# Attention and FP4 feed-forward on one core: who adds the partial denominators, and where the maximum enters the scores

## The chip, the cores and the metric

The kernel runs on one core of one Trainium2 chip. The metric is the device time of one execution in microseconds (us); lower is better. An execution has four engines that compute side by side, each with its own instruction stream: TensorE (PE in the profile, PEld for its weight loads), VectorE (DVE), ScalarE (ACT) and GpSimd (POOL). SyncE (SP) starts transfers. The streams meet only at semaphores: a wait such as `pe.wait_ge(p_ready, n)` holds back its own engine and everything queued behind it there.

## The reference, cut to what matters

```python
x = x + attention(layernorm(x))      # x is 1 x 2048 x 128, 16 heads of 64
x = x + ffn(layernorm(x))            # FP4 fake quantisation in blocks of 16, inner width 352
# attention:
sim  = einsum('bhid,bhjd->bhij', q, k) / 8
attn = softmax(sim, axis=-1)
out  = einsum('bhij,bhjd->bhid', attn, v)
```

All of it is float32. The change touches the softmax alone: its row maximum, which is subtracted before the exponential, and its denominator.

## The kernel before, in words

**Units.** The attention is cut into 32 units: 8 pairs of heads by 4 chunks of 512 queries. A unit has 16 steps j, one for each tile of 128 keys. The program text has 8 units (`BODY`), numbered w; they are run 4 times (`ITERS`), the last time with `last` set, and then without the projections for a next pair of heads and with parts of the feed-forward's quantisation in their place.

**A step.** PE makes the scores of 128 keys by 512 queries for two heads in one of the two buffers of `s_ps` (`scores`, L982 to L997), ACT takes the exponential of them into one of four buffers `probs` (L590), and PE multiplies these by V into `o_ps` (`weighted`, L1136). The scores come from split operands, three products for each of the two heads, and each product of a head uses 64 rows of the array; the two heads use different halves of it. The keys are held as differences to the tile two before, so a score buffer is not cleared within a unit: step j adds the difference to what step j-2 left. Only steps 0 and 1 (j < `BACK`) start a buffer, and there two products of a matrix of ones with `spread` add minus the row maximum, over all 128 rows of the array (L995). `spread` is a diagonal form of `neg_max`, written by DVE at L775 in step 13 for the unit after.

**Maxima.** Beside this, PE makes scores for the maxima of the unit ahead (`row_maxima`, L1002 and L1009, 64 rows for each of the two heads), ACT takes their positive part (`rise`, L510) and DVE folds both into `part_max` (`max_slot`, L766). Each of these has one buffer, so that PE's next `row_maxima` waits for DVE's last `max_slot` (`mx_free`) and ACT's last `rise` (`mx_rise`).

**Denominator.** POOL adds the probabilities of tiles 0 to 12 in 12 additions (L476) into `acc_pool`, DVE those of tiles 13 to 15 in two (L901, L906) into `acc_dve`. In step 1 of the next unit (`K_AT`) DVE adds the two into `acc_dve` (`sum_tiles`, L807), and in step 5 PE sums them over the partitions with a matrix of ones (`den`, L1118). The reciprocal (L784), the normalisation (L792), the output projection (L1126) and its addition to `y` (L799) follow.

**Order.** Every engine's order is written by hand. PE's is the loop at L1161 to L1177: in even steps `row_maxima` and then the scores of step j+1; in odd steps these scores and then `row_maxima`, then the projection due in this step (`misc`), then `weighted` for steps j-1 and j. In step 15 the scores are those of step 0 of the next unit. DVE's is the loop at L857 to L906, POOL's at L466 to L481. In the last four units POOL also scales inputs of the quantisation (`over_scale`, L452, after its additions; `times_scale`, L462), for which ACT waits in step 2 of the following unit (`sizes`, L570) and DVE supplies the factors (`block_scales`, L741, in step 15). ACT waits in each step for a free buffer of `probs`, that is for POOL's addition of four tiles before (`pool_free`).

Of the kernel before, what the change touches and what calls it, by code (L numbers as in the profile page):

```python
# [31 lines left out]
DH = 64  # L32
# [22 lines left out]
Q_BUFS = 4  # L55
# [84 lines left out]
def block_kernel(nc, x_in, w_qkv, w_out, b_out, w_gate, w_up, w_down, out):  # L140
    ctx = ExitStack()
    with ctx:
# [162 lines left out]
        def par(w):  # L305

            return (w // CHUNKS) % 2
# [94 lines left out]
        def _(pool):  # L402
# [36 lines left out]
                               ALU.add).then_inc(biased, 1)  # L439

            pool.wait_ge(dt_ready, CHUNKS)
            pool.memset(acc_dve[:, 1, :, :], 1.0).then_inc(dve_adds, DVE_ADDS - 1)
            pool.memset(acc_pool[:, 1, :, :], 0.0).then_inc(dve_adds, 1)
            pool.sem_inc(pool_adds, START)

            def over_scale(n):
                src, _dst, width = quantised(n)
# [17 lines left out]
            def body(it, last):  # L465
                for w in range(BODY):  # L466
                    acc = acc_pool[:, w % 2, :, :]
                    for j in range(1, POOL_TILES):
                        if j == 1:

                            pool.wait_ge(den_acc, after(it, 1, w))
                        else:
                            pool.wait_ge(pool_adds, after(it, POOL_ADDS, w, j - 1))
                        pool.wait_ge(p_ready, after(it, STEPS, w, j + 1))
                        first = probs[:, 0, :, :] if j == 1 else acc
                        pool.tensor_tensor(acc, first, probs[:, j % P_BUFS, :, :], ALU.add) \  # L476
                            .then_inc(pool_adds, 1)
                        if last and w > CHUNKS and j == 9:
                            times_scale(w - CHUNKS - 1)
                    if last and w >= CHUNKS:  # L480
                        over_scale(w - CHUNKS)  # L481

# [171 lines left out]
        def _(dve):  # L654
# [144 lines left out]
                dve.tensor_tensor(yc, yc, misc_ps[:, :].rearrange("p (t d) -> p t d", t=TQ), ALU.add) \  # L799
                    .then_inc(misc_free, 1)  # L800

            def sum_tiles(it, w):

                sums = acc_dve[:, (w - 1) % 2, :, :]
                dve.wait_ge(pool_adds, after(it, POOL_ADDS, w))
                dve.wait_ge(dve_adds, at(it, DVE_ADDS, w, DVE_ADDS))
                dve.tensor_tensor(sums, sums, acc_pool[:, (w - 1) % 2, :, :], ALU.add).then_inc(den_acc, 1)  # L807

            def split_weights(i, count):

                dve.wait_ge(wqkv_high, count)
# [42 lines left out]
            def body(it, last):  # L854
                for w in range(BODY):
                    sums = acc_dve[:, w % 2, :, :]
                    for j in range(STEPS):  # L857
# [3 lines left out]
                        if j == MAX_DONE and runs(last, u, s):  # L861
                            dve.wait_ge(s_ready, at(it, STEPS, w, BACK))
                            neg_maximum(max_no(it, w, j) + 1, at(it, 1, w, 2))
                        if j == K_AT:
                            sum_tiles(it, w)
                        if j == K_AT and not skipped("K", w, last):
                            dve.wait_ge(hi_done, kq_no(it, w, "K", last))
                            k_low(1 - par(w), w % CHUNKS, misc_ps[:, :]).then_inc(misc_free, 1)
# [39 lines left out]
            with dve.Fori(0, ITERS - 1) as it:  # L908
                body(it, False)
            body(ITERS - 1, True)  # L910
            sum_tiles(ITERS - 1, BODY)
            for t in range(TQ):
                invert(ITERS - 1, BODY, True, t)
            normalise(ITERS - 1, BODY, True)
# [41 lines left out]
        def _(pe):  # L956
# [22 lines left out]
                    ins = project_v_tile(ps, i, c, t)  # L979
                return ins  # L980

            def scores(buf, i, q, j, maximum=None):  # L982

                keys = slice(j * P, (j + 1) * P)
                parts = [(k_hi[i][:, keys], q_hi[q]), (k_hi[i][:, keys], q_lo[q]), (k_lo[i][:, keys], q_hi[q])]
                for n, (stationary, moving) in enumerate(parts):
                    for h in range(2):
                        rows = slice(DH * h, DH * (h + 1))
                        ins = pe.matmul(s_ps[:, buf, h, :], stationary[rows, :], moving[rows, :],  # L989
                                        start=(n == 0 and j < BACK), stop=(n == 2 and j >= BACK), skip_group_check=True)  # L990
                if j < BACK:
                    if maximum is not None:
                        pe.wait_ge(spread_ready, maximum)
                    for h in range(2):
                        ins = pe.matmul(s_ps[:, buf, h, :], ones_r[:, :], spread[:, h, :], start=False, stop=True,  # L995
                                        skip_group_check=True)
                return ins  # L997

            def base(h, i, k, q, pair):
# [82 lines left out]
            pe.wait_ge(zeros_ready, ZEROED)  # L1082
            pe.wait_ge(pro_v, CHUNKS)
            pe.wait_ge(pro_lo, len(PRO_LO))
            scores(0, 0, 0, 0, 1).then_inc(s_ready, 1)

            pe.sem_inc(pv_done, P_BUFS)

            def misc(name, it, w, last):
# [5 lines left out]
                if name == "raw":  # L1095
                    ins = project_raw(ps[:, 0:HALF], 1 - par(w), c)
                elif name == "K":
                    if c == 0:
                        pe.wait_ge(wqkv_split, it * 2 + w // CHUNKS + 2)
                    ins = project(ps, 1 - par(w), 1, c, dx_hi, dx_lo)  # L1100
                elif name == "V":
                    ins = project_v(ps, 1 - par(w), c)
                elif name == "Q":
                    ins = project(ps, par(w + 2), 0, (w + 2) % CHUNKS, xhat_hi, xhat_lo)
                elif name == "down":
                    for i, (row, rows) in enumerate(FF_TILES):
                        ins = pe.transpose(ps[0:rows, i * DIM:(i + 1) * DIM], wx[:, 6 * DIM + row:6 * DIM + row + rows],
                                           ident[:, :])
                elif name in ("gate", "up"):
                    pe.wait_ge(f_quant, 1)  # L1110
                    for i, (row, rows) in enumerate(FF_TILES):
                        col = (i if name == "gate" else 3 + i) * DIM
                        ins = pe.transpose(ps[:, row:row + rows], wx[0:rows, col:col + DIM], ident[0:rows, 0:rows])
                elif name == "den":

                    pe.wait_ge(den_acc, after(it, 1, w, 1))
                    for h in range(2):
                        ins = pe.matmul(ps[DH * h:DH * (h + 1), :], ones[:, :], acc_dve[:, (w - 1) % 2, h, :],  # L1118
                                        start=True, stop=True)
                else:  # L1120

                    if c == 1:
                        pe.wait_ge(wo_loaded[par(w)], it * 16 + 16)
                    pe.wait_ge(o_normed, after(it, 1, w, 2))
                    for t in range(TQ):
                        ins = pe.matmul(ps[:, t * P:(t + 1) * P], o_norm[:, t * P:(t + 1) * P], wo[par(w - 1)][:, :],  # L1126
                                        start=True, stop=True)
# [28 lines left out]
            def body(it, last):  # L1156
                for w in range(BODY):
                    ahead = not (last and w == BODY - 1)

                    pe.wait_ge(misc_free, misc_before(it, w, last) + START)  # L1160
                    for j in range(STEPS):  # L1161
                        if j % 2 == 0:
                            row_maxima(it, w, last, j)
                        if j < STEPS - 1:
# [1 line left out]
                            scores((j + 1) % 2, par(w), w % Q_BUFS, j + 1).then_inc(s_ready, 1)  # L1166
                        elif ahead:
                            pe.wait_ge(p_ready, after(it, STEPS, w, j))
                            scores(0, par(w + 1), (w + 1) % Q_BUFS, 0, at(it, 1, w, 2)).then_inc(s_ready, 1)
                        if j % 2:  # L1170
                            row_maxima(it, w, last, j)
                        if j in misc_at(w, last):
                            misc(misc_at(w, last)[j], it, w, last)
                        if j % 2:
# [77 lines left out]
```

## Time and profile before

| what | value |
|---|---|
| median of 3 runs | 1412.58 us (1411.9 to 1414.81) |
| the profiled execution, its time | 1419.41 us |
| its span, first to last instruction | 1417.6 us |
| mean granted TensorE clock | 0.972 of full speed |
| busy share of the span | PE 94%, PEld 48%, POOL 71%, DVE 69%, ACT 64% |

A row of the costliest groups or of a timeline has the engine, the line, the tiles written and read with their sizes, the count and the time. An engine's idle time before an instruction stands in brackets with the one that released it. PE's matrix products are pipelined: the length of one row overlaps the next one's, so that the cost of a product is read as the distance from its start to the next start. A row that says x2 holds the same product of both heads, which run side by side in the two halves of the array.

### The profile page before, as it was taken

What the parts mean: (1) busy time and instruction counts of PE and PEld (TensorE: products, weight loads), DVE (VectorE), ACT (ScalarE), POOL (GpSimd) and SP (SyncE); (2) the same over time, 40 slices, a digit from 0 to 9 for tenths busy, and PEclk for the clock granted to TensorE, in tenths of its full rate; (3) what the DMA queues carried; (4) which work ended last, traced back from release to release, by engine and by line L of the source; (5) the groups of instructions that cost most, each with busy time, mean ns of one, the idle gap of its engine ahead of it and who ended that gap; (6) DMA issues with size and microseconds to landing.
All of it is one profiled execution on the core that took longest, in us unless ns stands there. A gap on an engine that the chain in (4) does not pass through costs nothing.

```text
span 1417.6 us, 24287 instructions
## 1 busy us (share of the span) xinstructions
PE 1330.9 (94%) x7541; PEld 684.2 (48%) x7541; DVE 976.9 (69%) x2207; ACT 911.7 (64%) x1300; POOL 1007.8 (71%) x425
## 2 busy tenths in 40 slices
PE   5999999999999999999999999999999999899575
PEld 3555555544455454544445555454545554343245
DVE  6567766676667767677667676776766667878794
ACT  5566666766667666676666666666766677564242
POOL 4377778777677778877677777887777779797232
PEclk9799999999999999999999999999999999999687
DMA  2000000000000000000000000000000000000001
GB/s 60 1 8 1 1 1 9 1 1 1 3 9 1 1 1 9 1 1 1 3 9 1 1 1 9 1 1 1 1 3 1 1 1 0 1 1 1 0 1 30
DMA packets 9074, 6.41 MB, mean 5 GB/s; under 512 B 480, under 2 KB 8800, under 8 KB 8944
## 3 DMA queue, kind: packets, MB, share of 16 engines
q1 hardware_dynamic: 8720, 4.26, 1.1%
q8 instruction: 66, 1.08, 0.3%
q0 software_dynamic: 224, 0.54, 0.1%
q14 instruction: 64, 0.52, 0.1%
HBM read 3.75 MB, written 1.05 MB: 3 GB/s over the span
## 4 chain that ended last, share of the span: by engine, by line
PE 68%; issue 17%; DVE 11%; ACT 2%; POOL 1%; DMA 0%; DVEq 0%; POOLq 0%; ACTq 0%; SPq 0%
PE o_ps L1136 26%; PE s_ps L989 17%; PE mx_ps L1002 6%; PE mx_ps L1009 5%; DVE acc_dve L807 3%; PE misc_ps L1126 3%; PE misc_ps L1118 2%; PE s_ps L995 1%; ACT rise L510 1%; PE misc_ps L972 1%; PE misc_ps L960 1%; DVE k_lo L753 1%; PE s_ps L1218 1%; PE misc_ps L973 1%; PE misc_ps L974 1%
## 5 line engine op out<-in xcount | busy, mean ns | idle before, releaser
L476 POOL TENSOR_TENSOR acc_pool<-acc_pool,probs 128x1024 f32<-128x1024 f32 x352 | 878.1, 2495 | 48.5 <-POOL acc_pool L476 36.2
L590 ACT ACTIVATE probs<-s_ps 128x1024 f32<-128x1024 f32 x512 | 524.7, 1025 | 83.7 <-PE s_ps L989 29.2
L766 DVE CUSTOM_DVE_ANT_0 summed<-mx_ps,rise 128x512 bf16<-128x512 f32 x503 | 344.4, 685 | 327.7 <-issue 321.1
L510 ACT ACTIVATE rise<-mx_ps 128x512 f32<-128x512 f32 x503 | 300.3, 597 | 318.8 <-PE mx_ps L1009 270.4
L1136 PE MATMUL o_ps<-probs,vv 128*64 128x512 f32 x2048 | 497.5, 606 | 3.8 <-ACT probs L590 3.8
L476 POOL TENSOR_TENSOR acc_pool<-probs 128x1024 f32<-128x1024 f32 x32 | 77.2, 2412 | 261.7 <-ACT probs L590 261.7
L1009 PE MATMUL mx_ps<-k_hi,q_hi 64*128 64x512 f32 x503 | 231.1, 459 | 18.5 <-DVE part_max L766 17.4
L1002 PE MATMUL mx_ps<-k_raw,q_hi 64*128 64x512 f32 x503 | 232.3, 462 | 4.9 <-issue 3.3
L1136 PEld LDWEIGHTS o_ps<-probs,vv 128*64 128x64 f32 x2048 | 127.1, 136 | 224.0 <-issue 180.7
L989 PE MATMUL s_ps<-q_hi,k_hi 64*128 64x512 f32 x1024 | 207.4, 401 | 1.1 <-ACT probs L590 1.0
L989 PE MATMUL s_ps<-q_hi,k_lo 64*128 64x512 f32 x1024 | 202.4, 391 | 0.0
L989 PE MATMUL s_ps<-q_lo,k_hi 64*128 64x512 f32 x1024 | 202.0, 390 | 0.0
L1002 PEld LDWEIGHTS mx_ps<-k_raw,q_hi 64*128 64x128 f32 x503 | 92.9, 185 | 206.7 <-issue 206.2
L784 DVE RECIPROCAL rden<-misc_ps 128x128 f32<-128x128 f32 x132 | 120.9, 938 | 11.7 <-PE misc_ps L1118 11.7
L1009 PEld LDWEIGHTS mx_ps<-k_hi,q_hi 64*128 64x128 f32 x503 | 93.0, 185 | 53.9 <-issue 45.4
L989 PEld LDWEIGHTS s_ps<-q_hi,k_hi 64*128 64x128 f32 x1024 | 97.1, 186 | 32.2 <-issue 19.0
L989 PEld LDWEIGHTS s_ps<-q_hi,k_lo 64*128 64x128 f32 x1024 | 96.7, 185 | 22.3
L989 PEld LDWEIGHTS s_ps<-q_lo,k_hi 64*128 64x128 f32 x1024 | 96.9, 185 | 20.4
L775 DVE TENSOR_TENSOR spread<-ident,neg_max 128x1024 fp32r<-128x1024 f32 x32 | 96.4, 3011 | 1.1
L807 DVE TENSOR_TENSOR acc_dve<-acc_dve,acc_pool 128x1024 f32<-128x1024 f32 x33 | 92.9, 2815 | 0.2
L995 PE MATMUL s_ps<-spread,ones_r 128*128 128x512 f32 x128 | 48.0, 457 | 2.1 <-DVE spread L775 2.1
L792 DVE TENSOR_TENSOR o_norm<-o_raw,rden 128x512 f32<-128x512 f32 x33 | 49.8, 1508 | 0.1
(162 smaller groups left out, 1165.0 us busy)
## 6 DMA issues: line engine op xcount, KB each, us to landing
wqkv<-in_L_attn_w_qkv SPq DMA_DIRECT2D x8, 192.0 KB, 2.7
y<-in_L_attn_x SPq DMA_DIRECT2D x4, 256.0 KB, 4.2
out<-y SPq DMA_DIRECT2D x4, 256.0 KB, 2.3
wo<-in_L_attn_w_out SPq DMA_DIRECT2D x8, 64.0 KB, 1.9
wx<-in_L_ffn_w_down POOLq DMA_DIRECT2D x1, 176.0 KB, 5.7
wx<-in_L_ffn_w_gate POOLq DMA_DIRECT2D x1, 128.0 KB, 4.2
wx<-in_L_ffn_w_up POOLq DMA_DIRECT2D x1, 128.0 KB, 5.0
bias<-in_L_attn_b_out SPq DMA_DIRECT2D x1, 64.0 KB, 5.6
```

The costliest lines, as they stand in the source:

```text
L476: pool.tensor_tensor(acc, first, probs[:, j % P_BUFS, :, :], ALU.add) \
L510: act.activation(rise[:, h, :], mx_bank(h, pair), ACT.Relu).then_inc(mx_rise, 1)
L590: act.activation(probs[:, j % P_BUFS, :, :], s_ps[:, j % 2, :, :], ACT.Exp, scale=SCALE) \
L766: dve.tensor_tensor_reduce(summed[:, s % 2, :], mx_bank(h, pair), rise[:, h, :], 1.0, LOWEST, ALU.add, ALU.max, part_max[:, slot:slot + 1] ...
L775: dve.tensor_tensor(spread[:, :, :].rearrange("p h (t q) -> p (h t) q", q=P), ident[:, :].unsqueeze(1).to_broadcast([P, 2 * TQ, P]), neg_m ...
L784: ins = dve.reciprocal(rden[:, cols], misc_ps[:, cols])
L807: dve.tensor_tensor(sums, sums, acc_pool[:, (w - 1) % 2, :, :], ALU.add).then_inc(den_acc, 1)
L989: ins = pe.matmul(s_ps[:, buf, h, :], stationary[rows, :], moving[rows, :], start=(n == 0 and j < BACK), stop=(n == 2 and j >= BACK), skip ...
L995: ins = pe.matmul(s_ps[:, buf, h, :], ones_r[:, :], spread[:, h, :], start=False, stop=True, skip_group_check=True)
L1002: return pe.matmul(mx_bank(h, pair), q_hi[q][rows, t * P:(t + 1) * P], k_raw[k][rows, g * QC:(g + 1) * QC], start=True, stop=True)
L1009: return pe.matmul(mx_bank(h, pair).rearrange("p (c n) -> p c n", n=HALF), q_hi[q][rows, t * P:(t + 1) * P], moving, start=True, stop=True)
L1136: ins = pe.matmul(o_ps[DH * h:DH * (h + 1), :], vv[par(w)][:, j, DH * h:DH * (h + 1)], probs[:, j % P_BUFS, h, :], start=(j == 0), stop=(j ...
```

## The change

POOL, not DVE, adds the two partial denominators, at the end of its own unit and into `acc_pool`; it waits for DVE's second addition first. `den` reads `acc_pool`. DVE's `sum_tiles` is gone, in all its 33 places (32 units, and a first one over constants); POOL has 32. One of the two constants is set in `acc_pool` in place of `acc_dve`, and the other is no longer written.

The products with `spread` become a function `maxima`. For the first buffer they come behind `row_maxima` of step 15; for the second they open the buffer at the start of step 0, ahead of `row_maxima` and the scores.

```diff
             pool.wait_ge(dt_ready, CHUNKS)
-            pool.memset(acc_dve[:, 1, :, :], 1.0).then_inc(dve_adds, DVE_ADDS - 1)
-            pool.memset(acc_pool[:, 1, :, :], 0.0).then_inc(dve_adds, 1)
+            pool.memset(acc_pool[:, 1, :, :], 1.0).then_inc(den_acc, 1)
             pool.sem_inc(pool_adds, START)
+            pool.sem_inc(dve_adds, DVE_ADDS)
...
-                            pool.wait_ge(den_acc, after(it, 1, w))
+                            pool.wait_ge(den_acc, after(it, 1, w, 1))
...
+                    pool.wait_ge(pool_adds, after(it, POOL_ADDS, w, POOL_ADDS))
+                    pool.wait_ge(dve_adds, at(it, DVE_ADDS, w, 2 * DVE_ADDS))
+                    pool.tensor_tensor(acc, acc, acc_dve[:, w % 2, :, :], ALU.add).then_inc(den_acc, 1)
                     if last and w >= CHUNKS:
                         over_scale(w - CHUNKS)
...
-            def sum_tiles(it, w):
-
-                sums = acc_dve[:, (w - 1) % 2, :, :]
-                dve.wait_ge(pool_adds, after(it, POOL_ADDS, w))
-                dve.wait_ge(dve_adds, at(it, DVE_ADDS, w, DVE_ADDS))
-                dve.tensor_tensor(sums, sums, acc_pool[:, (w - 1) % 2, :, :], ALU.add).then_inc(den_acc, 1)
...
-                        if j == K_AT:
-                            sum_tiles(it, w)
...
-            def scores(buf, i, q, j, maximum=None):
+            def maxima(buf, start):
+
+                for h in range(2):
+                    ins = pe.matmul(s_ps[:, buf, h, :], ones_r[:, :], spread[:, h, :], start=start, stop=not start,
+                                    skip_group_check=True)
+                return ins
+
+            def scores(buf, i, q, j):
...
-                                        start=(n == 0 and j < BACK), stop=(n == 2 and j >= BACK), skip_group_check=True)
-                if j < BACK:
-                    if maximum is not None:
-                        pe.wait_ge(spread_ready, maximum)
-                    for h in range(2):
-                        ins = pe.matmul(s_ps[:, buf, h, :], ones_r[:, :], spread[:, h, :], start=False, stop=True,
-                                        skip_group_check=True)
+                                        start=(n == 0 and j == 0), stop=(n == 2 and j > 0), skip_group_check=True)
                 return ins
...
                     for j in range(STEPS):
+                        if j == 0:
+                            pe.wait_ge(p_ready, after(it, STEPS, w))
+                            maxima(1, True)
                         if j % 2 == 0:
                             row_maxima(it, w, last, j)
...
-                            scores(0, par(w + 1), (w + 1) % Q_BUFS, 0, at(it, 1, w, 2)).then_inc(s_ready, 1)
+                            scores(0, par(w + 1), (w + 1) % Q_BUFS, 0)
                         if j % 2:
                             row_maxima(it, w, last, j)
+                        if j == STEPS - 1 and ahead:
+                            pe.wait_ge(spread_ready, at(it, 1, w, 2))
+                            maxima(0, False).then_inc(s_ready, 1)
```

## Rows read from the trace of the kernel before

**Rows 1.** The profile's page: busy time, share of the span, instructions, by engine.

```profile
PE 1330.9 (94%) x7541; PEld 684.2 (48%) x7541; DVE 976.9 (69%) x2207; ACT 911.7 (64%) x1300; POOL 1007.8 (71%) x425
```

**Rows 2.** Waits of PE, whole span: us in total, times, longest us.

```profile
PE mx_ps L1009 <- DVE part_max L766: 17.4, 34, 4.3
```

**Rows 3.** Timeline of PE, 642 to 654 us: start us, duration us, instruction [idle before].

```profile
642.09 0.39 PE L989 MATMUL s_ps<-q_hi,k_lo 64*128 64x512 f32 x2
642.41 0.74 PE L995 MATMUL s_ps<-spread,ones_r 128*128 128x512 f32 x2
643.07 0.50 PE L1009 MATMUL mx_ps<-k_hi,q_hi 64*128 64x512 f32 x1
...
643.50 1.94 PE L1136 MATMUL o_ps<-probs,vv 128*64 128x512 f32 x8
...
646.50 0.73 PE L995 MATMUL s_ps<-spread,ones_r 128*128 128x512 f32 x2
647.16 0.50 PE L989 MATMUL s_ps<-q_hi,k_hi 64*128 64x512 f32 x2
647.50 0.39 PE L989 MATMUL s_ps<-q_lo,k_hi 64*128 64x512 f32 x2
647.73 0.40 PE L989 MATMUL s_ps<-q_hi,k_lo 64*128 64x512 f32 x2
...
653.28 0.46 PE L1009 MATMUL mx_ps<-k_hi,q_hi 64*128 64x512 f32 x1 [0.36 <-DVE part_max L766]
```

**Rows 4.** Timeline of DVE, 638 to 652 us.

```profile
638.36 3.08 DVE L775 TENSOR_TENSOR spread<-ident,neg_max 128x1024 fp32r<-128x1024 f32 x1
641.38 0.68 DVE L766 CUSTOM_DVE_ANT_0 summed<-mx_ps,rise 128x512 bf16<-128x512 f32 x1
...
644.24 1.22 DVE L906 TENSOR_TENSOR acc_dve<-acc_dve,probs 128x1024 f32<-128x1024 f32 x1
...
649.01 2.90 DVE L807 TENSOR_TENSOR acc_dve<-acc_dve,acc_pool 128x1024 f32<-128x1024 f32 x1
```

**Rows 5.** Line L775 on DVE: duration ns min/median/max, first and last start us.

```profile
L775 DVE TENSOR_TENSOR spread<-ident,neg_max x32: 1226/3312/3368, 48.5 to 1274.9; 128x1024 fp32r<-128x1024 f32 x32
```

**Rows 6.** Timeline of POOL, 638 to 654 us.

```profile
638.00 2.36 POOL L476 TENSOR_TENSOR acc_pool<-acc_pool,probs 128x1024 f32<-128x1024 f32 x1 [0.16 <-POOL acc_pool L476]
648.45 2.38 POOL L476 TENSOR_TENSOR acc_pool<-probs 128x1024 f32<-128x1024 f32 x1 [8.09 <-ACT probs L590]
650.99 3.17 POOL L476 TENSOR_TENSOR acc_pool<-acc_pool,probs 128x1024 f32<-128x1024 f32 x1 [0.16 <-POOL acc_pool L476]
```

**Rows 7.** Timeline of POOL at the last three unit boundaries.

```profile
1192.70 2.95 POOL L452 TENSOR_TENSOR scaled<-wx,binv 128x1120 f32<-128x1120 f32 x1 [0.76 <-DVE binv L741]
1197.52 2.37 POOL L476 TENSOR_TENSOR acc_pool<-probs 128x1024 f32<-128x1024 f32 x1 [1.87 <-ACT probs L590]
...
1244.11 2.37 POOL L476 TENSOR_TENSOR acc_pool<-probs 128x1024 f32<-128x1024 f32 x1 [1.57 <-ACT probs L590]
...
1283.13 1.91 POOL L452 TENSOR_TENSOR scaled<-fx,binv 128x512 f32<-128x512 f32 x1 [6.70 <-DVE binv L741]
1285.01 3.34 POOL L476 TENSOR_TENSOR acc_pool<-probs 128x1024 f32<-128x1024 f32 x1
```

**Rows 8.** Line L452 on POOL: duration ns min/median/max, first and last start us.

```profile
L452 POOL TENSOR_TENSOR scaled<-fx,binv x4: 1058/1909/1914, 1240.6 to 1341.9; 128x512 f32<-128x512 f32 x4
```

**Rows 9.** Waits of ACT for POOL, 1080 to 1330 us.

```profile
ACT probs L590 <- POOL acc_pool L476: 14.6, 10, 2.3
```

**Rows 10.** Timeline of DVE, the last sum.

```profile
1322.93 1.88 DVE L807 TENSOR_TENSOR acc_dve<-acc_dve,acc_pool 128x1024 f32<-128x1024 f32 x1
```

**Rows 11.** Windows: length, busy (instructions) of PE PEld DVE ACT POOL, PEclk, DMA, GB/s.

```profile
1231.00:1237.00 6.00, 1.03 (x4) 0.62 (x4) 5.66 (x18) 0.99 (x1) 2.87 (x1) 0.77 0.00 1
1237.00:1241.00 4.00, 4.00 (x10) 0.77 (x8) 3.93 (x11) 1.51 (x2) 0.38 (x1) 0.50 0.00 0
1241.00:1246.00 5.00, 5.00 (x30) 2.29 (x30) 3.20 (x8) 4.03 (x6) 3.43 (x2) 1.00 0.00 0
```

More of the change, by code:

```diff
@@ L910, in _ @@
             body(ITERS - 1, True)
-            sum_tiles(ITERS - 1, BODY)
             for t in range(TQ):
@@ L1084, in _ @@
             pe.wait_ge(pro_lo, len(PRO_LO))
-            scores(0, 0, 0, 0, 1).then_inc(s_ready, 1)
+            scores(0, 0, 0, 0)
+            pe.wait_ge(spread_ready, 1)
+            maxima(0, False).then_inc(s_ready, 1)
             pe.sem_inc(pv_done, P_BUFS)
@@ L1117, in misc @@
                     for h in range(2):
-                        ins = pe.matmul(ps[DH * h:DH * (h + 1), :], ones[:, :], acc_dve[:, (w - 1) % 2, h, :],
+                        ins = pe.matmul(ps[DH * h:DH * (h + 1), :], ones[:, :], acc_pool[:, (w - 1) % 2, h, :],
                                         start=True, stop=True)
@@ L1168, in body @@
                             pe.wait_ge(p_ready, after(it, STEPS, w, j))
-                            scores(0, par(w + 1), (w + 1) % Q_BUFS, 0, at(it, 1, w, 2)).then_inc(s_ready, 1)
+                            scores(0, par(w + 1), (w + 1) % Q_BUFS, 0)
                         if j % 2:
                             row_maxima(it, w, last, j)
+                        if j == STEPS - 1 and ahead:
+                            pe.wait_ge(spread_ready, at(it, 1, w, 2))
+                            maxima(0, False).then_inc(s_ready, 1)
                         if j in misc_at(w, last):
```

## The prediction, made before the changed kernel ran

> **What bounds the kernel now.** I read the engines' busy shares first: PE is busy 94% of the span, the next engine 71% [rows 1]. An engine that full is the bound of most of the span, so I look for two things alone: where PE waits, and where its products cost more than their columns. The waits of PE have one entry that the change can reach in every unit, `row_maxima` waiting for DVE's `part_max`, 17.4 us in 34 places [rows 2].
>
> The timeline of one unit boundary shows its cause and the other cost. The reader is to see starts, not durations. Between pairs of the same 64-row shape the starts lie 0.23 us apart (647.50 to 647.73). Where the shape changes they do not: from the last pair of scores to the products with `spread`, which use all 128 rows, it is 0.32 (642.09 to 642.41), and from the first pair behind them to the next 0.34 (647.16 to 647.50). `row_maxima` of step 15, a single pair between two other shapes, takes 0.43 (643.07 to 643.50) [rows 3]. So leaving the 64-row shape costs some 0.09 and returning to it 0.11: **0.20 us for each block of another shape that stands between 64-row products**. On DVE the sum of the denominators starts at 649.01 and takes 2.90, where an addition of the same size took 1.22 [rows 4]. POOL's addition ran until 650.83 (648.45 plus 2.38), and POOL's next, which ran beside the sum, took 3.17 instead of some 2.37 [rows 6]. The two engines take turns, and DVE's `max_slot` of step 2, behind the sum, is late: PE waits 0.36 for it at 653.28 [rows 3].
>
> **Part 1, the sum leaves DVE.** PE's 0.36 us goes in each of the 28 units before the last four and the first of these four. I count 0.35 times 29, **10.2 us**; the remaining 7 of the 17.4 lie in the last three units, where DVE has the quantisation as well, and I count nothing for them. What is late next: with 2.90 us less ahead of it, `max_slot` of step 2 starts when its input is there, as in the other steps, where PE doesn't wait.
>
> POOL gets 32 additions of 2.4 us. In most units they cost nothing: POOL stands idle for 8.09 us ahead of its first addition of a unit [rows 6]. DVE's last addition ends at 645.46 (644.24 plus 1.22) [rows 4]; the sum then ends by 647.9, ahead of 648.45, when ACT's probabilities let POOL go on. With part 2 both ends come some 0.3 earlier. Queued behind the waiting POOL is only its own next addition; the one who waits for the sum is `den`, in step 5, some 10 us on. Without that cover the price would be up to 2.4 us a unit, but POOL would have to lose over 5 us of slack in a unit first. POOL's second addition also falls from 3.17 to some 2.37, so its later ones come 0.8 earlier. Removed with it are one sum and one constant ahead of the loop, beside PE work: zero.
>
> **Part 2, the order on PE.** Before: scores, `spread`, `row_maxima` 15, weighted, `row_maxima` 0, scores, `spread`, scores, `row_maxima` 1. After: scores, `row_maxima` 15, `spread`, weighted, `spread`, `row_maxima` 0, scores, scores, `row_maxima` 1. No product is added; two blocks that broke up 64-row work now lie against the weighted products, which break it up anyway. That is 2 times 0.20, **0.40 us** a boundary, if a change between the 128-row and the weighted shape stays as dear as the change from 64 rows that it replaces. Below, it could be 0.18 (only the 0.09 is saved twice) or zero; above, nothing beyond 0.43 speaks. I take 0.40, since it comes from this very place. 28 boundaries up to the last four units: 11.2, and with the very first unit's single block **11.4 us**. The new wait for the exponential of step 15 costs nothing: the weighted product ahead of it waits for the same. ACT's first exponential of a unit stands behind its `rise` of step 15, which now comes earlier.
>
> Here something is nearly late. `row_maxima` 15 moves to 642.32 (642.09 plus 0.23) and needs DVE's `max_slot` of step 14, done at 642.06 (641.38 plus 0.68) plus some 0.1 for its signal: 0.1 to 0.2 to spare [rows 3, 4]. That slot starts behind `spread`, which took 3.08 here and 3.31 in the median unit [rows 4, 5], which would make it 0.1 late. But `spread` is long because it waits for POOL's addition begun at 638.00 [rows 6], and this begins 0.8 earlier for POOL, 0.4 earlier against PE. So I expect no wait.
>
> The two engines also take turns over the new additions. On the rows, DVE's `spread` and its sum waited out POOL's addition, and POOL's next one waited for the sum; `max_slot`, which has one input in PSUM, took 0.68 beside the end of POOL's, as ever [rows 4, 6]. While POOL makes the new sum in a main unit, DVE has `max_slot` alone, so I count zero; in the last units DVE has other work there, which is a rival below.
>
> **Part 3, the last units.** There POOL's `over_scale` stands in the idle time, and the sum is put ahead of it. DVE's last addition comes behind the factors that `over_scale` waits for.
> - First boundary: two DVE additions and a slot (1.2, 0.7, 1.2 with gaps: 2.8) and the sum's 2.4 come first, +5.2; `over_scale` then loses its collision, 2.95 to some 2.1 [rows 7, 8], and the idle 1.87 is used up [rows 7]: +2.5. The collision with DVE's sum goes, -0.8: **+1.7**.
> - Second: 1.2 and 2.4, less 0.85, less the idle 1.57 [rows 7], less 0.8: **+0.4**.
> - Third: 1.2 and 2.4, less 0.85, no idle [rows 7], less 0.96 (3.34 to 2.38): **+1.8**.
> - End: the last sum is exposed. DVE's took 1.88 [rows 10], POOL's will take 2.4: **+0.5**.
>
> POOL sets the pace there, since ACT waits for its additions, 14.6 us in 10 places [rows 9], so these count in full and the gains of part 2 at these boundaries not at all: +4.4 together (0 to 9: nothing if PE's own gains cover them; twice that if ACT's wait for `over_scale` in step 2 adds its own).
>
> **Sum.** -10.2 - 11.4 + 4.4 = -17.2 us. The profiled execution took 1419.4 and would take 1402.2; the median of the runs shown is 6.8 lower, and I take the same difference from it: 1412.6 - 17.2 = **1395.4**.
>
> **The rivals.**
> - *The shapes pay less.* If `row_maxima` 15 waits for DVE, or the changes against the weighted product cost what was saved, part 2 falls to between 0 and 0.26 a boundary. For it: the 0.1 us of slack. Against it: POOL's earlier phase. 1412.6 - 10.2 - 7.5 + 4.4 = 1399 with 0.26 left of it, and 1407 with nothing.
> - *POOL's delay is absorbed.* The last units have PE waits of their own, which the earlier work may fill: part 3 falls to 0, 1391.
> - *POOL holds DVE in the last units.* There DVE has instructions with two SBUF inputs for the quantisation. If each of the four new additions holds one of them for its 2.4 us, on a path that counts, 4 x 2.4 = 9.6 us come on top: 1405. For it: the turns taken at 649.01. Against it: between DVE's last addition and step 2 the quantisation has nothing for DVE. The Trainium skill ("SBUF — State Buffer", "SBUF: two separate sides") has the rule behind this: DVE and GpSimd share one pair of ports under an exclusive lock, and a DVE instruction with two SBUF inputs and a GpSimd instruction that reads SBUF block each other for the whole of an instruction. By that rule this rival holds wherever the two meet, and the rows of the main units agree with it (2.90 against 1.22).
> - *The clock, the slow side.* PE was busy 1.03 of the 6 us from 1231, and in the next 4 the granted clock was 0.50 (1.2 instead of 2.4 GHz), then 1.00 again [rows 11]. More delay on POOL lengthens such pauses. If the clock stays at its lower level from there through the next unit, PE's work in it, some 37 us (94% of a unit of 39 to 40 [rows 1]), takes 74, and the kernel ends near 1395 + 74 - 40 = 1429. It decides once some 17 us of PE work more run at the lower level. Against it: the clock was back within 4 us of full work.
> - *The change doesn't do what it says:* the wait of 0.36 might really be ACT's. Then part 1 gives nothing and the time is 1406. The row's releaser and the 2.90 speak against it.
>
> **How the numbers follow.** Forecast 0.60; shapes pay less 0.15; absorbed 0.11; the wait isn't DVE's 0.04; POOL holds DVE 0.03; both gains missing together, near 1413 or a little above, 0.03; the clock 0.04. A measurement of this kernel can tell 0.2%, 2.8 us. All but the last two lie below 1409.8: faster 0.93, same 0.03, slower 0.04. The range takes in the forecast with its bounds of a few us, the absorbed case and the nearer end of the first rival, and leaves out some 0.18: 1389 to 1403.
>
> **What would show it.** In the changed trace: no wait for `part_max` at step 2 in the main units; unit boundaries 0.75 us closer together (28 units, 21 us); the starts of step 15's `row_maxima` 0.23 behind the last scores; POOL's idle before its first addition split into a wait for DVE's addition, a sum of 2.4 and under 1 us; DVE's `spread` below 3 us. In the last units POOL's first additions come up to 2.5 us later against the unit. A wait of `row_maxima` 15, POOL's first addition held by the sum, or the clock at 0.5 ahead of 1310 us would make the prediction wrong.

## The result, and the profile after

The changed kernel takes **1391.76 us** (median; 1391.6 to 1393.47), the kernel before 1412.59 beside it: a ratio of 0.9853, with a 95% interval of 0.9836 to 0.9870 (each ratio below has such an interval behind it). The forecast was 1395.4, with a range of 1389 to 1403. The gain was 20.8 us where 17.2 were forecast.

The page of the changed kernel, its span and its busy times:

```profile
span 1388.8 us, 24313 instructions
...
PE 1307.2 (94%) x7541; PEld 683.4 (49%) x7541; DVE 886.8 (64%) x2174; ACT 909.5 (65%) x1300; POOL 1057.5 (76%) x456
```

PE keeps its 94% of a shorter span, with the same 7541 products [rows 1]. DVE is 90 us less busy, POOL 50 us more. Three of the costliest groups (busy us, mean ns of one | idle time before them and what ended it):

```profile
L482 POOL TENSOR_TENSOR acc_pool<-acc_pool,acc_dve 128x1024 f32<-128x1024 f32 x32 | 76.3, 2386 | 150.6 <-DVE acc_dve L900 150.6
...
L476 POOL TENSOR_TENSOR acc_pool<-probs 128x1024 f32<-128x1024 f32 x32 | 75.9, 2371 | 52.6 <-ACT probs L593 52.5
...
L778 DVE TENSOR_TENSOR spread<-ident,neg_max 128x1024 fp32r<-128x1024 f32 x32 | 88.7, 2772 | 1.1
```

The sum is L482 now, 2386 ns each, and the wait for DVE's addition takes most of POOL's former idle time ahead of its first addition. `spread` takes 2772 ns on average, 240 less than before. The wait of PE that stood in rows 2:

```profile
PE mx_ps L1003 <- DVE part_max L769: 9.1, 4, 5.9
```

Only four waits are left in this list, all in the last units. Their count fell by 30, but by their total only 8.3 us went with them, and the time fell by 21.

**One unit boundary**, on PE, then DVE, then POOL (start us, duration us, instruction, idle before). These answer to rows 3, 4 and 6.

```profile
623.56 0.39 PE L989 MATMUL s_ps<-q_hi,k_lo 64*128 64x512 f32 x2
623.78 0.40 PE L1003 MATMUL mx_ps<-k_hi,q_hi 64*128 64x512 f32 x1
...
624.12 0.73 PE L978 MATMUL s_ps<-spread,ones_r 128*128 128x512 f32 x2
624.78 1.94 PE L1132 MATMUL o_ps<-probs,vv 128*64 128x512 f32 x8
626.65 0.73 PE L978 MATMUL s_ps<-spread,ones_r 128*128 128x512 f32 x2
627.32 0.50 PE L996 MATMUL mx_ps<-k_raw,q_hi 64*128 64x512 f32 x1
...
627.65 0.40 PE L989 MATMUL s_ps<-q_hi,k_hi 64*128 64x512 f32 x2
...
628.35 0.39 PE L989 MATMUL s_ps<-q_hi,k_hi 64*128 64x512 f32 x2
...
629.04 0.39 PE L996 MATMUL mx_ps<-k_raw,q_hi 64*128 64x512 f32 x1
```

```profile
619.84 3.08 DVE L778 TENSOR_TENSOR spread<-ident,neg_max 128x1024 fp32r<-128x1024 f32 x1
622.86 0.68 DVE L769 CUSTOM_DVE_ANT_0 summed<-mx_ps,rise 128x512 bf16<-128x512 f32 x1
```

```profile
619.47 2.37 POOL L476 TENSOR_TENSOR acc_pool<-acc_pool,probs 128x1024 f32<-128x1024 f32 x1 [0.16 <-POOL acc_pool L476]
626.52 2.40 POOL L482 TENSOR_TENSOR acc_pool<-acc_pool,acc_dve 128x1024 f32<-128x1024 f32 x1 [4.67 <-DVE acc_dve L900]
629.74 2.37 POOL L476 TENSOR_TENSOR acc_pool<-probs 128x1024 f32<-128x1024 f32 x1 [0.82 <-ACT probs L593]
632.27 2.40 POOL L476 TENSOR_TENSOR acc_pool<-acc_pool,probs 128x1024 f32<-128x1024 f32 x1 [0.16 <-POOL acc_pool L476]
```

The reader is to see the starts again. `row_maxima` 15 begins 0.22 us behind the last scores, the products with `spread` 0.34 behind it, the weighted ones 0.66 behind these; the second `spread` block 1.87 behind those; then `row_maxima` 0, scores, scores and `row_maxima` 1 run through at 0.33 and 0.23. The two blocks have gone to the weighted products. POOL's sum starts at 626.52, ends at 628.92, and leaves 0.82 us of idle time; its second addition (632.27) takes 2.40 in place of 3.17. But `spread` on DVE still takes 3.08, and POOL's twelfth addition begins 0.37 ahead of it, as before (0.36 [rows 4, 6]). At this boundary `row_maxima` 15 was in time all the same; at 14 others it was not, as the experiments show.

**Where the time went.** I measure a unit from POOL's first addition in it (the group `acc_pool<-probs`) to the first addition of the next. The table, worked out from the starts of these 32 rows, gives the distances in us; "28 units" ends at the start of the last four.

| kernel | to the first | 28 units | w4, w5, w6 | w7 to `den` | rest | span |
|---|---|---|---|---|---|---|
| before | 57.8 | 1102.5 | 37.3, 46.6, 40.9 | 40.0 | 92.6 | 1417.6 |
| changed | 51.1 | 1079.1 | 38.7, 46.6, 42.6 | 39.5 | 91.2 | 1388.8 |

The spans differ by 28.8 us and the medians by 20.8. Most of the difference is the column to the first addition: in the profiled execution of before the granted clock was lower there. The windows of before, then of the changed kernel (start:end, length, busy of PE, PEld, DVE, ACT and POOL, clock):

```profile
40.00:50.00 10.00, 10.00 (x35) 6.55 (x34) 5.63 (x21) 4.63 (x9) 0.00 (x0) 0.50 0.01 2
50.00:60.00 10.00, 9.99 (x39) 4.80 (x39) 4.56 (x13) 6.53 (x10) 2.24 (x1) 0.67 0.00 0
```

```profile
40.00:50.00 10.00, 9.69 (x58) 6.24 (x57) 7.88 (x29) 7.57 (x14) 0.00 (x0) 1.00 0.01 2
```

The change is not what made the difference: in the profiled executions of the experiments below the first addition comes at 49.5 to 51.2 us, and at 50.7 where only one line differs from the kernel before. The stretch at 0.50 of full speed cost 6.6 us, and the profiled execution of before was 6.8 above its median. Without it the spans differ by 22.2: 23.4 gained in 28 units, 2.7 given back from there to `den`, and 1.5 gained behind it. This last part varies from 90.9 to 94.1 us over all the kernels profiled here, so that a difference of 1.5 us there shows nothing. Of the 28 distances in the changed kernel 14 are 38.43 to 38.48 us (39.15 to 39.21 before; I call these the typical units), 6 are 38.58 to 38.61 (39.5 before; there DVE also splits new weights), 6 are 38.01 to 38.16, and two have the loop's own end in them.

### The profile page after: what moved, and what is told of

It reads as the page before. It is cut to its first block, busy times and chain, and to the rows that moved or that the text cites. A ratio compares the mean times of both kernels' runs of the same rounds, so it can differ in the third digit from the quotient of the medians.

```text
span 1388.8 us, 24313 instructions
## 1 busy us (share of the span) xinstructions
PE 1307.2 (94%) x7541; PEld 683.4 (49%) x7541; DVE 886.8 (64%) x2174; ACT 909.5 (65%) x1300; POOL 1057.5 (76%) x456
## 3 DMA queue, kind: packets, MB, share of 16 engines
q1 hardware_dynamic: 8720, 4.26, 1.1%
## 4 chain that ended last, share of the span: by engine, by line
PE 84%; DVE 7%; issue 5%; POOL 2%; ACT 1%; DMA 0%; POOLq 0%; SPq 0%; ACTq 0%; DVEq 0%
PE o_ps L1132 31%; PE s_ps L989 24%; PE mx_ps L996 8%; PE mx_ps L1003 4%; PE s_ps L978 3%; PE misc_ps L1122 3%; PE misc_ps L1114 2%; PE misc_ps L953 2%; PE misc_ps L965 1%; POOL acc_pool L476 1%; PE misc_ps L954 1%; PE misc_ps L955 1%; PE misc_ps L966 1%; PE misc_ps L967 1%; DVE split L715 1%
## 5 line engine op out<-in xcount | busy, mean ns | idle before, releaser
L476 POOL TENSOR_TENSOR acc_pool<-acc_pool,probs 128x1024 f32<-128x1024 f32 x352 | 857.3, 2435 | 49.4 <-POOL acc_pool L476 38.3
L1003 PE MATMUL mx_ps<-k_hi,q_hi 64*128 64x512 f32 x503 | 225.2, 448 | 11.6 <-DVE part_max L769 9.1
L996 PE MATMUL mx_ps<-k_raw,q_hi 64*128 64x512 f32 x503 | 226.1, 449 | 1.4 <-DVE part_max L769 1.2
L989 PE MATMUL s_ps<-q_hi,k_hi 64*128 64x512 f32 x1024 | 204.2, 394 | 0.9 <-ACT probs L593 0.4
L482 POOL TENSOR_TENSOR acc_pool<-acc_pool,acc_dve 128x1024 f32<-128x1024 f32 x32 | 76.3, 2386 | 150.6 <-DVE acc_dve L900 150.6
L989 PEld LDWEIGHTS s_ps<-q_hi,k_lo 64*128 64x128 f32 x1024 | 97.0, 185 | 22.2
L778 DVE TENSOR_TENSOR spread<-ident,neg_max 128x1024 fp32r<-128x1024 f32 x32 | 88.7, 2772 | 1.1
```

The source lines that it names most:

```text
L482: pool.tensor_tensor(acc, acc, acc_dve[:, w % 2, :, :], ALU.add).then_inc(den_acc, 1)
L778: dve.tensor_tensor(spread[:, :, :].rearrange("p h (t q) -> p (h t) q", q=P), ident[:, :].unsqueeze(1).to_broadcast([P, 2 * TQ, P]), neg_m ...
L996: return pe.matmul(mx_bank(h, pair), q_hi[q][rows, t * P:(t + 1) * P], k_raw[k][rows, g * QC:(g + 1) * QC], start=True, stop=True)
L1003: return pe.matmul(mx_bank(h, pair).rearrange("p (c n) -> p c n", n=HALF), q_hi[q][rows, t * P:(t + 1) * P], moving, start=True, stop=True)
```

## The experiments

A unit gained 0.7 to 1.1 us, where I had 0.75. Theory A, formed from these distances: the late `max_slot` had cost PE the shift of its starts and the loss of the weights loaded ahead, 0.63 us and not 0.36; and the new order gains its 0.40, of which a new wait of `row_maxima` 15 eats 0.28 in most units. Theory B: the wait was worth its 0.36, and the order more than 0.40.

### The sum alone, and the order alone

The sum alone has the lines of POOL and DVE from the change and PE's order of before, with one edit on PE, in `den`:

```diff
-                        ins = pe.matmul(ps[DH * h:DH * (h + 1), :], ones[:, :], acc_dve[:, (w - 1) % 2, h, :],
+                        ins = pe.matmul(ps[DH * h:DH * (h + 1), :], ones[:, :], acc_pool[:, (w - 1) % 2, h, :],
```

The order alone has PE's other lines from the change, and POOL and DVE as before:

```diff
+                        if j == 0:
+                            pe.wait_ge(p_ready, after(it, STEPS, w))
+                            maxima(1, True)
...
+                        if j == STEPS - 1 and ahead:
+                            pe.wait_ge(spread_ready, at(it, 1, w, 2))
+                            maxima(0, False).then_inc(s_ready, 1)
```

> Only the sum is moved to POOL; PE keeps the order of before. Theory A (the late max_slot costs PE the shift of its starts, 0.52 us, and 0.11 more for a first pair whose weights were not loaded ahead, 0.63 in all, where the profile's idle time says 0.36): a typical unit goes from 39.17 to 38.54 us, 28 units give 17.6 us, and the last four units give back 1 to 3: 1396 to 1398 us. Theory B (the wait is worth the 0.36 of the profile, and the order is worth more than 0.40): a typical unit 38.81, and 1403 to 1405 us.

> Only the order on PE is changed; the sum stays on DVE. Theory A (0.40 us a boundary less a new wait of row_maxima 15 for DVE's max_slot 14, some 0.24 with the weights not loaded ahead, as spread still takes 3.3 us): a typical unit from 39.17 to 39.01, the whole 1408 us (1406 to 1410). Theory B (the order is worth what the wait does not explain): a typical unit below 38.85 and at most 1403 us.

The sum alone: **1397.09 us**, ratio 0.9889 (0.9873 to 0.9906). Typical unit 38.56, 28 units 1083.8 us: 18.7 less than before. Theory A.

The order alone: **1411.24 us**, ratio 0.9986 (0.9977 to 0.9996). It gained less than both theories said. Typical unit 39.20, where before had 39.17; only the main units of the last pass fell, to 38.93. PE's waits for `part_max`:

```profile
PE mx_ps L1010 <- DVE part_max L766: 25.0, 35, 3.8
```

They grew from 17.4 to 25.0 us. At one of them, PE and then DVE:

```profile
643.78 0.40 PE L996 MATMUL s_ps<-q_hi,k_lo 64*128 64x512 f32 x2
644.72 0.47 PE L1010 MATMUL mx_ps<-k_hi,q_hi 64*128 64x512 f32 x1 [0.55 <-DVE part_max L766]
```

```profile
640.26 3.09 DVE L807 TENSOR_TENSOR acc_dve<-acc_dve,acc_pool 128x1024 f32<-128x1024 f32 x1
```

Between the last pair of scores and `row_maxima` 3 there are 0.94 us of starts, which with all in time would be 0.23. The sum, begun at 640.26, took 3.09. Before, these starts were 0.75 apart. So of the 0.40 us, the half that PE saves between POOL's first addition and this place becomes a longer wait: while the sum stands in step 1 of DVE, its end sets PE's pace there. The other half goes at `row_maxima` 15, in a typical unit:

```profile
554.95 0.39 PE L996 MATMUL s_ps<-q_hi,k_lo 64*128 64x512 f32 x2
555.31 0.47 PE L1010 MATMUL mx_ps<-k_hi,q_hi 64*128 64x512 f32 x1
555.74 0.73 PE L985 MATMUL s_ps<-spread,ones_r 128*128 128x512 f32 x2
```

It begins 0.36 behind the last scores in place of 0.23, and takes 0.43 in place of 0.32, 0.24 together, as theory A had for this wait. Theory A lacked the other loss, 0.19. In the last pass POOL's additions follow one another without the 0.16 us of idle time between them, `spread` takes 2.6 us and `row_maxima` 15 is in time; there a part of the gain is left. So the parts do not add up: 16.2 and 2.1 us alone (before took 1413.33 beside them), 20.8 together.

### One block more, and the first maximum back

One block more:

```diff
-                        if j == 0:
-                            pe.wait_ge(p_ready, after(it, STEPS, w))
-                            maxima(1, True)
                         if j % 2 == 0:
                             row_maxima(it, w, last, j)
+                        if j == 0:
+                            pe.wait_ge(p_ready, after(it, STEPS, w))
+                            maxima(1, True)
```

The first maximum back:

```diff
                             scores(0, par(w + 1), (w + 1) % Q_BUFS, 0)
+                            pe.wait_ge(spread_ready, at(it, 1, w, 2))
+                            maxima(0, False).then_inc(s_ready, 1)
                         if j % 2:
                             row_maxima(it, w, last, j)
-                        if j == STEPS - 1 and ahead:
-                            pe.wait_ge(spread_ready, at(it, 1, w, 2))
-                            maxima(0, False).then_inc(s_ready, 1)
```

> The changed kernel with the maximum of the second buffer behind row_maxima 0 in place of ahead of it: the same products, and one block of 64-row products more that stands between other shapes. Theory A (0.09 on leaving and 0.11 on entering the 64-row shape): +0.20 us in each of 28 to 32 units, +5.6 to +6.4, 1397 to 1398 us. Rival (the border costs nothing and the order gained by taking row_maxima 15 off a wait): within 1 us of the changed kernel's 1391.8.

> The changed kernel with the maximum of the first buffer directly behind its scores again, that of the second still opening its sum. Theory A (in the changed kernel row_maxima 15 waits for max_slot 14, which costs 0.28 us in the units where spread takes 3.1 to 3.4 us): the block costs 0.20, the wait goes, all units 38.36 us between boundaries, those that had 38.44 a little shorter and those that had 38.16 longer: 1391 to 1393 us. Rival (no wait there; the 0.28 between units belongs to something else): every unit 0.20 longer, 1397 us.

One block more: **1397.57 us** (0.9893, 0.9876 to 0.9909). The units of the last pass have 38.36 or 38.37 where the changed kernel has 38.16. **A block costs 0.20 us.** The first maximum back: **1393.59 us** (0.9858, 0.9842 to 0.9875), 0.6 above what theory A gave, but with its units: nearly every one of 38.45 and of 38.16 has 38.37 now. So one of the two moved blocks was worth nothing in the typical units, since the wait took it back. The wait itself can be read in the changed kernel, one typical unit and then one without it:

```profile
546.18 0.39 PE L989 MATMUL s_ps<-q_hi,k_lo 64*128 64x512 f32 x2
546.63 0.47 PE L1003 MATMUL mx_ps<-k_hi,q_hi 64*128 64x512 f32 x1
...
547.07 0.73 PE L978 MATMUL s_ps<-spread,ones_r 128*128 128x512 f32 x2
```

```profile
1047.72 0.39 PE L989 MATMUL s_ps<-q_hi,k_lo 64*128 64x512 f32 x2
1047.95 0.39 PE L1003 MATMUL mx_ps<-k_hi,q_hi 64*128 64x512 f32 x1
...
1048.27 0.74 PE L978 MATMUL s_ps<-spread,ones_r 128*128 128x512 f32 x2
```

From the last scores to `row_maxima` 15 it is 0.45 in the one and 0.23 in the other, and then 0.44 in place of 0.32. The loads of the pair's weights show why: with the wait they come 0.03 ahead of the product, without it 0.22.

```profile
546.60 0.18 PEld L1003 LDWEIGHTS mx_ps<-k_hi,q_hi 64*128 64x128 f32 x1 [0.46 <-issue]
...
1047.73 0.18 PEld L1003 LDWEIGHTS mx_ps<-k_hi,q_hi 64*128 64x128 f32 x1
```

No row of PE has an idle time in brackets for it, because the modelled end of the last scores (546.18 plus 0.39) covers all but 0.06 of it. `spread` in that unit:

```profile
542.46 3.41 DVE L778 TENSOR_TENSOR spread<-ident,neg_max 128x1024 fp32r<-128x1024 f32 x1
```

### Fewer tiles for POOL

```diff
-POOL_TILES = 13
+POOL_TILES = 12
```

> The changed kernel with one tile less for POOL (12 in place of 13) and one more for DVE. Theory A (row_maxima 15 waits for max_slot 14 because spread waits out POOL's twelfth addition): POOL is done some 2.5 us before spread starts, spread takes 1.2 us in every unit, the 0.28 goes in 19 units (5.3 us), all units 38.16 but the one in four with the weight split; POOL's shorter chain gives 1 to 5 us in the last four units: 1382 to 1386 us. Rival (DVE is the bound there, and one more addition of 1.2 us in step 13 makes max_slot 14 as late as before): no change in the main units, 1388 to 1393 us.

**1385.07 us** (0.9804, 0.9787 to 0.9822). `spread`'s durations (ns, least/median/most), in the changed kernel and in this one:

```profile
L778 DVE TENSOR_TENSOR spread<-ident,neg_max x32: 1224/3109/3409, 45.3 to 1245.4; 128x1024 fp32r<-128x1024 f32 x32
```

```profile
L778 DVE TENSOR_TENSOR spread<-ident,neg_max x32: 1224/1225/2596, 43.8 to 1240.7; 128x1024 fp32r<-128x1024 f32 x32
```

POOL is done some 0.5 us before `spread` starts, and the third addition on DVE does no harm: typical unit 38.16, the least in this order. The 28 units take 1076.1 us, 3.0 less where theory A had 5.3; one of them has 39.44, for a reason that I did not look for. The wait of `row_maxima` 15 came from the meeting of `spread` with POOL's twelfth addition.

### The sum on DVE after all, a step earlier

```diff
-                        if j == K_AT:
+                        if j == 0:
                             sum_tiles(it, w)
```

> The kernel before with DVE's sum in step 0 of the next unit in place of step 1, nothing on POOL and nothing on PE. Theory A (the sum is dear only because it meets POOL's first addition of the unit; in step 0 POOL is idle): the sum takes 1.2 us in place of 2.8, PE's wait in step 2 goes, a typical unit 38.54 to 38.56, 28 units give 17 us and the last ones nothing back: 1395 to 1397 us. Rival (DVE is simply short of time at the unit boundary, and only taking the sum away helps): a wait in step 0 or 1 takes its place, 1405 us or more.

> As the run before, with the new order on PE. Theory A (the gains add up as in the changed kernel): typical units 38.2 to 38.5, and no sum on POOL in the last four units: 1388 to 1392 us. Rival (the order gains nothing without the sum off DVE, as in the run with the order alone): 1395 us or more.

The kernel before with this one line: **1390.65 us** (0.9853, 0.9836 to 0.9870), as good as the whole change and 4 us below what theory A gave.

```profile
L807 DVE TENSOR_TENSOR acc_dve<-acc_dve,acc_pool x33: 1215/1222/1887, 48.9 to 1294.7; 128x1024 f32<-128x1024 f32 x33
```

The same 33 sums, median 1222 ns in place of 2895. Typical unit 38.56, to the hundredth what the sum on POOL gave. **The cost was the meeting, not the work.** The sum is also a step earlier here, which alone would have helped PE, and no run has a short sum in step 1 of the main units; but the 1.7 us by which the meeting lengthens the sum are more than the 0.52 by which PE's starts were late. The last units gain as well: w4, w5, w6 take 36.4, 45.0 and 41.0 us, 122.4 together, where the sum on POOL in the same order takes 127.7. Some of this is the clock: at the end of w5 PE waits 2.10 us at the longest, and the granted clock stays at 1.00, where in the kernel before a wait of 4.26 us was followed by 0.50. With the new order: **1388.30 us** (0.9828, 0.9808 to 0.9848), typical units 38.45 to 38.50 and 38.16 in the last pass, as theory A said; but w5 takes 48.9 us.

### The scaling ahead of the sum

```diff
+                    if last and w >= CHUNKS:
+                        over_scale(w - CHUNKS)
                     pool.wait_ge(pool_adds, after(it, POOL_ADDS, w, POOL_ADDS))
...
-                    if last and w >= CHUNKS:
-                        over_scale(w - CHUNKS)
```

> The changed kernel with over_scale ahead of the sum in the last four units. Main units as in the changed kernel. Theory A (the sum ahead of over_scale makes ACT wait for it in step 2, and PE with it): the wait of ACT for POOL's over_scale falls from 9.8 to under 5 us, and 1 to 3 us are gained: 1389 to 1391 us. Rival (POOL's own chain is the bound there, whichever comes first): within 1 us of 1391.8.

**1388.47 us** (0.9845, 0.9821 to 0.9868). As a time this lies below what either theory gave, but the kernel before took 1412.24 beside it, and the ratio is not to be told apart from the changed kernel's 0.9853. ACT's waits for POOL, in the changed kernel and then in this one:

```profile
ACT probs L593 <- POOL acc_pool L476: 13.7, 15, 2.3
...
ACT scaled L573 <- POOL scaled L452: 9.8, 7, 3.9
```

```profile
ACT probs L593 <- POOL acc_pool L476: 19.2, 17, 3.4
...
ACT scaled L573 <- POOL scaled L452: 3.8, 6, 1.4
```

The wait for `over_scale` fell by 6.0 us and that for POOL's additions rose by 5.5. From w4 to `den` the changed kernel takes 167.4 us (167.5 in a second profiled execution), this one 167.2. The rival holds: POOL's chain is the bound there, whichever comes first.

### The best version

> Sum on DVE in step 0, new order on PE, 12 tiles for POOL. Theory A (both meetings of DVE and POOL are gone, the sum's and spread's, and POOL has no new addition): main units 38.16 (one in four 38.5), 2.6 us less than with 13 tiles over 28 units, and 1 to 3 us less in the last four: 1383 to 1386 us. Rival (DVE, with all sums and one more addition, becomes the bound at the boundary): 1388 us or more.

> The changed kernel with 12 tiles for POOL and over_scale ahead of the sum. If the two gains add up (6.7 and 3.3 us): 1382 us (1380 to 1384). If the second is inside the first, since POOL's shorter chain already hides the wait: 1385 us.

> The changed kernel again, beside the two above on the same chip: 1391 to 1392 us, main units 38.44 to 38.47.

Run side by side: the sum on DVE in step 0, the new order and 12 tiles for POOL **1381.95 us** (0.9777, 0.9763 to 0.9791); the changed kernel with 12 tiles and the scaling first 1383.26 (0.9787, 0.9772 to 0.9803), too near to the 0.9804 of 12 tiles alone to say whether the scaling adds anything; the changed kernel 1391.98 (0.9844, 0.9830 to 0.9858), its typical units 38.40 to 38.48 but for two of 39.15 and 38.96. The first, 1 us below what its theory gave, beats both the kernel before and the changed one, 10 us below the changed one, and POOL has no sum in it. Its page:

```profile
span 1381.6 us, 24295 instructions
...
PE 1303.2 (94%) x7541; PEld 681.7 (49%) x7541; DVE 907.6 (66%) x2239; ACT 908.1 (66%) x1300; POOL 906.0 (66%) x393
```

POOL is 152 us less busy than in the changed kernel, and its 28 units take 1074.7 us.

## Why the prediction was right, and where it was off

**The sum leaves DVE: right in its mechanism, its size too small.** The step "I count 0.35 times 29, 10.2 us" took the idle time in brackets for the cost. 28 units gave 18.7 us (the sum alone), a typical one 0.61. The trace of before had it: the last scores ahead of the `row_maxima` at 653.28 start at 652.53, 0.75 before it where 0.23 is usual, which is 0.52 lost, and this pair takes 0.43 to the next start in place of 0.32, 0.63 together. With the sum gone from step 1 the two distances are 0.23 and 0.32. The bracket counts only from the modelled end of the product before, 0.16 us behind the moment at which the next could have started. That it was the meeting, and not the amount of DVE's work, is shown by the sum in step 0. One reading under this step was wrong without harm: the `max_slot` that "took 0.68 beside the end of POOL's" starts at 641.38, when POOL's addition had been over since 640.36 [rows 4, 6]; one that does lie beside an addition of POOL, at 652.44, takes 0.68 as well.

**The order: right for each block, wrong in "So I expect no wait".** 0.20 us a block is shown three times: changed kernel against one block more (38.16, 38.36), against the first maximum back (38.16, 38.37), and, for two blocks, the sum alone against the changed kernel without the wait (38.56, 38.16). But `row_maxima` 15 did wait, some 0.28 us in 14 typical units. I had POOL's additions 0.8 us earlier and PE only 0.4, hence 0.4 to spare. In the typical unit shown above, PE and DVE now take 28.26 us from POOL's first addition to `spread`, where they took 29.08 in the same unit of before, and POOL takes 28.23 to its twelfth in place of 28.99: 0.82 and 0.76 less, so that the two met as before, and `spread` took 3.41 us in place of 3.35. It is the mis-sized term again. Over 28 units the order gave 4.7 us (1083.8 to 1079.1) in place of 11.4; a second profiled execution of the changed kernel had 1081.4, so that this gain is known to some 2 us. The one error was 8.5 too low and the other 6.7 too high. That they nearly cancel is luck, and the forecast stands nearer than its steps: with both sizes right it would have been 1393.6, but with only one of them right 1402 or 1387, ten us above the measurement or five below it.

**The parts depend on each other**, which no step of mine said: the order alone gives 2 us of its 11, since the sum on DVE paces one half of the boundary and `row_maxima` 15 waits in the other.

**The signs.** Of those that I had named, the wait at step 2 is gone in the main units, and POOL's idle time is split as I had it. But `spread` below 3 us did not come in most units (median 3.11), and the wait of `row_maxima` 15, which I had said would make the prediction wrong, did: that step failed, whatever the total.

**The cover of POOL's sum: right.** It ends 0.8 us ahead of the next addition, which I had put under 1 us.

**The last units: right at the boundaries, too dear in sum.** I had +1.7, +0.4 and +1.8, and +0.5 at the end. At the three boundaries, one after the other, POOL's rows show the sum, `over_scale` behind it and the first addition:

```profile
1164.51 2.38 POOL L482 TENSOR_TENSOR acc_pool<-acc_pool,acc_dve 128x1024 f32<-128x1024 f32 x1 [3.67 <-DVE acc_dve L900]
1166.85 2.10 POOL L452 TENSOR_TENSOR scaled<-wx,binv 128x1120 f32<-128x1120 f32 x1
1168.91 2.35 POOL L476 TENSOR_TENSOR acc_pool<-probs 128x1024 f32<-128x1024 f32 x1
...
1212.00 2.39 POOL L482 TENSOR_TENSOR acc_pool<-acc_pool,acc_dve 128x1024 f32<-128x1024 f32 x1 [7.89 <-DVE acc_dve L900]
1214.35 1.07 POOL L452 TENSOR_TENSOR scaled<-fx,binv 128x512 f32<-128x512 f32 x1
1215.51 2.38 POOL L476 TENSOR_TENSOR acc_pool<-probs 128x1024 f32<-128x1024 f32 x1
...
1254.78 2.38 POOL L482 TENSOR_TENSOR acc_pool<-acc_pool,acc_dve 128x1024 f32<-128x1024 f32 x1 [7.84 <-DVE acc_dve L900]
1257.12 1.06 POOL L452 TENSOR_TENSOR scaled<-fx,binv 128x512 f32<-128x512 f32 x1
1258.14 2.35 POOL L476 TENSOR_TENSOR acc_pool<-probs 128x1024 f32<-128x1024 f32 x1
```

`over_scale` takes 2.10, 1.07 and 1.06 us in place of 2.95, 1.91 and 1.91 [rows 7, 8], as I had it. w4 to w6 took 3.2 us more than before (127.95 to 124.77), where the three terms had 3.9. At the end PE's wait for the last sum grew from 7.0 to 7.5 us, as forecast, but w7 up to there was 0.5 shorter all in all. What I had not seen is that the same three would have been 2.4 shorter than before with the sum in DVE's step 0: in the profiled executions the sum on POOL takes 5.4 us more there. Not all of that is POOL's: 1.5 of it lies in w5, where the clock stayed at 1.00 with the sum in step 0.

**The rivals.** "The shapes pay less" was half right, by the wait that it named, and its 0.1 us of slack were the sign. "The clock" did not happen: PE's pause at the end of w5 lasts 5.91 us, the products behind it run at half speed (the eight weighted ones take 3.61 us in place of 1.87), and the next block is at full speed again. POOL's exclusive turns with DVE cost nothing at the place of the new sum, as forecast. At two other places the median of an instruction with two SBUF inputs fell from 2895 to 1222 ns (the sum) and from 3109 to 1225 (`spread`) once POOL was idle beside it; the rule of the Trainium skill ("SBUF — State Buffer", "SBUF: two separate sides"), that such an instruction and a reading GpSimd instruction block each other, agrees with both.

**Left open.** w5 takes 48.8 to 48.9 us in the three kernels with the new order and the sum on DVE, and 45.0 to 47.0 in all others. The traces tell a part of it. These are windows behind the pause at the end of w5, with the sum in step 0 and PE's old order, and with the new order:

```profile
1211.00:1217.00 6.00, 5.44 (x32) 2.28 (x30) 5.93 (x14) 4.06 (x7) 3.10 (x2) 1.00 0.00 0
```

```profile
1204.00:1210.00 6.00, 5.58 (x13) 1.68 (x13) 5.27 (x14) 1.62 (x2) 1.66 (x1) 0.50 0.00 0
```

PE's wait for `part_max` is 2.10 us in the first and 3.78 in the second, and what follows runs at 1.00 in the one and at 0.50 in the other, where 6 us hold 32 rows of products in the one and 13 in the other. The other two of the three wait 3.5 and 3.8 us there and are at 0.50 as long. But the changed kernel waits 5.91 us at this place and its w5 takes 46.6, so that neither the wait nor the clock is the whole of it. The rest was not tried.

## What to carry to other kernels

Ahead of moving work off an engine, see whether it is long or only waits for a neighbour: moved by one step, away from POOL's instruction, the sum cost DVE 1.2 us in place of 2.9, and one line did what the whole change did. Price a wait of TensorE by the distance of the starts around it, not by its idle time, and use the same price for what else moves with it. And when one engine gains time, work out again where it meets the others: a gain may bring back the meeting that it was to avoid.

## What the runs showed that I had not expected

- The profile's idle time of PE was short of the real cost of a wait by 0.27 us (0.36 against 0.63), and a start that was 0.22 us late had no bracket at all (546.63).
- A pair of products behind a wait takes 0.11 us more than in a full stream, 0.44 against 0.32, the same as behind a change of shape.
- The same DVE instruction with two SBUF inputs (128x1024) took 1.22 us beside an idle POOL and up to 3.4 beside a busy one, while those with one input in PSUM (`max_slot`) took 0.68 to 0.69 in both cases.
